# Two products of a gated delta-rule recurrence, computed as 64x64 tiles of TensorE

## The reference, cut to what matters

```python
def step(M, inp):
    q_t, k_t, v_t, b_t, g_t = inp
    M = M * jnp.exp(g_t)[..., None, None]
    Mk = jnp.einsum('bhd,bhdv->bhv', k_t, M)
    M = M + jnp.einsum('bhd,bhv->bhdv', k_t, (v_t - Mk) * b_t[..., None])
    o_t = jnp.einsum('bhd,bhdv->bhv', q_t, M)
    return (M, o_t)
```

## Time and profile before

| | |
|---|---|
| Three runs | 2204.56, 2207.28 and 2207.43 us, median 2207.28 us |
| Profiled execution, span | 2206.9 us |
| Mean granted TensorE clock | 0.989 of full speed |
| Busy: PE, PEld | 2103.0 us (95%), 1734.9 us (79%) |
| Busy: DVE, ACT, POOL | 1242.6 us (56%), 988.4 us (45%), 814.4 us (37%) |

### The profile page before, as it was taken

The page is one execution under the profiler, slowest core; times in us unless marked ns, Lnnn a source line. Parts: engine busy times, 40 slices in busy tenths (PEclk is TensorE's granted clock), DMA queues, the critical chain, the costliest instruction groups (busy, mean ns, idle before and its releaser), DMA issues.

```text
span 2206.9 us, 37731 instructions
## 1 busy us (share of the span) xinstructions
PE 2103.0 (95%) x12418; PEld 1734.9 (79%) x12418; DVE 1242.6 (56%) x2160; ACT 988.4 (45%) x3083; POOL 814.4 (37%) x1169
## 2 busy tenths in 40 slices
PE   5899999999999999999999999999999799999999
PEld 4688888888988888888888888888898665757574
DVE  5656565656666656566565656565666544343434
ACT  2455454546364646454555545464636331212111
POOL 2254453535353636353545445353535200000000
PEclk9899999999999999999999999999999989999999
DMA  2011111101010101010101111111102340403020
GB/s 93 15 34 26 29 36 21 31 21 35 22 38 14 38 19 38 14 38 15 37 21 31 29 24 36 21 31 21 36 21 63 125 128 10 115 16 109 19 57 19
DMA packets 220091, 85.37 MB, mean 39 GB/s; under 512 B 138320, under 2 KB 204240, under 8 KB 219280
## 3 DMA queue, kind: packets, MB, share of 16 engines
q1 hardware_dynamic: 220048, 84.83, 15.2%
HBM read 57.28 MB, written 27.53 MB: 38 GB/s over the span
## 4 chain that ended last, share of the span: by engine, by line
PE 72%; issue 12%; DVE 9%; ACT 3%; POOL 2%; DMA 1%; POOLq 0%; DVEq 0%; SPq 0%; ACTq 0%
PE bank L515 27%; PE bank L683 5%; PE bank L670 5%; PE bank L771 4%; PE bank L708 3%; PE bank L635 3%; PE bank L728 2%; PE bank L735 2%; PE bank L714 2%; PE bank L719 2%; PE bank L734 2%; PE bank L702 2%; DVE vT L1316 2%; PE bank L588 1%; PE bank L834 1%
## 5 line engine op out<-in xcount | busy, mean ns | idle before, releaser
L515 PE MATMUL bank<-x_hi,w_hi 128*128 128x512 f32 x1024 | 422.6, 413 | 18.3 <-DVE w_lo L1263 11.6
L515 PE MATMUL bank<-x_hi,w_lo 128*128 128x512 f32 x1024 | 409.5, 400 | 0.0
L515 PE MATMUL bank<-x_lo,w_hi 128*128 128x512 f32 x1024 | 408.5, 399 | 0.0
L515 PEld LDWEIGHTS bank<-x_hi,w_hi 128*128 128x128 f32 x1024 | 194.0, 189 | 60.0 <-issue 16.2
L515 PEld LDWEIGHTS bank<-x_hi,w_lo 128*128 128x128 f32 x1024 | 193.8, 189 | 36.7
L515 PEld LDWEIGHTS bank<-x_lo,w_hi 128*128 128x128 f32 x1024 | 194.5, 190 | 31.3
L1316 DVE SCALAR_TENSOR_TENSOR qT<-bank,cw,qT 128x511 f32<-128x511 f32 (+2 forms) x192 | 143.4, 747 | 82.7 <-ACT qT L954 78.1
L1316 DVE SCALAR_TENSOR_TENSOR vT<-bank,cw,vT 128x511 f32<-128x511 f32 (+2 forms) x192 | 143.2, 746 | 44.8 <-ACT vT L954 40.3
L1707 POOL TENSOR_TENSOR o_rstd<-o_ms,minus_half 128x4 f32<-128x4 f32 x64 | 70.7, 1104 | 258.1 <-DVE o_ms L1395 258.1
L1739 POOL TENSOR_TENSOR rstd<-ve,mhalf 128x1 f32<-128x1 f32 x32 | 17.4, 543 | 387.6 <-DVE ve L1479 387.6
L1114 ACT ACTIVATE o_tmp<-bank 128x128 f32<-128x128 f32 x256 | 67.4, 278 | 201.5 <-PE bank L735 201.5
(11 more groups left out here) (219 smaller groups left out, 4860.6 us busy)
## 6 DMA issues: line engine op xcount, KB each, us to landing
w_raw<-in_w_heads SPq DMA_DIRECT2D x64, 256.0 KB, 2.8
o_d<-og SPq DMA_DIRECT2D x64, 256.0 KB, 2.6
o_raw<-o_d SPq DMA_DIRECT2D x16, 1024.0 KB, 6.1
x_in<-in_x SPq DMA_DIRECT2D x16, 256.0 KB, 3.4
blkN_d<-nT SPq DMA_DIRECT2D x64, 64.0 KB, 2.0
t<-blkT_d SPq DMA_DIRECT2D x64, 64.0 KB, 2.4
wo_raw<-in_w_out SPq DMA_DIRECT2D x4, 1024.0 KB, 7.9
x_res<-in_x SPq DMA_DIRECT2D x16, 256.0 KB, 2.7
```

The lines of the kernel that those rows point to most:

```text
L515: last = mm(bank[bk][:, :], w[:, kind % 2, d, :], xx[:, d, b * S:(b + 1) * S], start=(n == 0), stop=(n == 3 * ND - 1))
```

## The change

The two products, L714 and L719, use only the blocks that matter: L714 takes the 64 rows of the early half and the 64 columns of the late half of `nT`, and L719 takes the late half of `tT` both ways. Each matmul's weights become 64x64, its moving operand 64 rows x 128 columns, and its result the upper 64 partitions of the bank. The copy to `vv` and the subtraction from `w1` work on those 64 partitions. The memsets, their three waits, and TensorE's wait for them go. An instruction that only adds 1 to a semaphore is put on TensorE before each of the two products, behind the wait for the copy.

```diff
+EARLY, LATE = slice(0, P // 2), slice(P // 2, P)
@@ semaphores: x2_only goes, "pe" comes to held @@
@@ TensorE, one chunk of the recurrence @@
                     pe.wait_ge(w1_done, 4 * h + c + 1)
-                    pe.wait_ge(x2_only, 2 * h + 2)
+                    hold(pe, "pe")
                     for b in range(B):
-                        last = mm(grid(2)[:, b, :], nT[:, b, c, :], w1[:, c % 2, b, :], start=True, stop=True)
+                        last = mm(grid(2)[LATE, b, :], nT[EARLY, b, c, LATE], w1[EARLY, c % 2, b, :], start=True, stop=True)
                     last.then_inc(v_mm, 1)
                     ahead(fill[2])
                     pe.wait_ge(vv_done, 4 * h + c + 1)
+                    hold(pe, "pe")
                     for b in range(B):
-                        last = mm(grid(3)[:, b, :], tT[:, b, c, :], vv[:, b, :], start=True, stop=True)
+                        last = mm(grid(3)[LATE, b, :], tT[LATE, b, c, LATE], vv[LATE, b, :], start=True, stop=True)
@@ ScalarE @@
-                    fn(vv[:, :, :], grid(2), ACT.Copy).then_inc(vv_done, 1)
+                    fn(vv[LATE, :, :], grid(2)[LATE], ACT.Copy).then_inc(vv_done, 1)
@@ VectorE @@
-                    tt(w1[:, c % 2, :, :], w1[:, c % 2, :, :], grid(3), ALU.subtract).then_inc(w_done, 1)
+                    tt(w1[LATE, c % 2, :, :], w1[LATE, c % 2, :, :], grid(3)[LATE], ALU.subtract).then_inc(w_done, 1)
@@ GpSimd @@
-                pool.wait_ge(x1_done, 4 * h + 4)
-                pool.wait_ge(x0_done, 4 * h + 4)
-                pool.wait_ge(qg_done, 3 * h + 3)
-                hold(pool, "pool")
-                for i in range(2):
-                    s = i * P // 2
-                    memset(nT[s:s + P // 2, :, :, s:s + P // 2], 0.0).then_inc(x2_only, 1)
-                    pool.wait_ge(x2_only, 2 * h + i + 1)
-                    if i == 0:
-                        hold(pool, "pool")
```

More of the change, by code:

```diff
@@ L287, in layer @@
         sem(n) for n in ("blkT_zero", "blkN_out", "blkN_in", "inv_set", "sub_step", "blkT_out", "t32_in", "tT_done", "t32_done"))
-    x0_done, x1_done, y_mrg, y_copied, z_mrg, merged, x2_only = (
-        sem(n) for n in ("x0_done", "x1_done", "y_mrg", "y_copied", "z_mrg", "merged", "x2_only"))
+    x0_done, x1_done, y_mrg, y_copied, z_mrg, merged = (
+        sem(n) for n in ("x0_done", "x1_done", "y_mrg", "y_copied", "z_mrg", "merged"))
     ks_mm, rhs_done, w1_mm, w1_done, v_mm, vv_done, tv_mm, w_done, sg_done, s_mm, s_done = (
@@ L315, in layer @@
     heads_over = [sem(f"heads_over_{e}") for e in ("pe", "act", "dve", "pool")]
-    held = {"dve": sem("dve_held"), "pool": sem("pool_held"), "sp": sem("sp_held")}
+    held = {"pe": sem("pe_held"), "dve": sem("dve_held"), "pool": sem("pool_held"), "sp": sem("sp_held")}
     def hold(engine, name):
```

## The result

The changed kernel takes 2231.49 us (median of 4 runs, 2226.84 to 2234.40) against 2207.02 us (median of 4 runs of the kernel before, the three above and one more). The ratio is 1.0112, with a 95% interval of 1.0097 to 1.0126: slower by 24.5 us. The profiled execution has a span of 2231.1 us, 24.2 more than before, and a time of 2233.03 us.

What follows compares the result with a forecast made beforehand. TensorE, 95% busy, bounds it, with the product-copy chain as long as the fill beside it. Added instruction +8.4 less shorter loads 6.0 gives +2.4; with shape changes +9.7 to +44.8, middle +27: 2206.9 + 27, 2234 us; range 2200 to 2258.

Steps and rivals of the forecast that it cites:

- The stall at the change of shape: Between fill and products, four shape changes a chunk, 240 in 15 heads, drain TensorE; sum between +9.7 and +44.8 us.
- the middle between two ends 35 us apart: Shape-change cost taken midway between +9.7 us (load merely cannot overlap) and +44.8 us (load waits for the record's end): +27.
- Entry: From fill to product, the product begins later: +0.04 to +0.19 us in 105 products, -0.04 to +0.11 in 15.
- Exit: From product back to fill, the fill's load finishes later: +0.10 to +0.28 us in each of 120 products.
- The added instruction: Semaphore increment ahead of L714 and L719: 0.08 us in 105 products, 8.4 us; nothing beside a draining array.
- Memsets, copy and subtraction at 0: Removing GpSimd's 32 memsets and cutting copy L1108 and subtraction L1408 to 64 partitions gains 0 on the path.
- What the waits hide: Exits after L719 partly covered by existing waits: 5.9 us off the lower end, 10.4 us off the upper.
- the last head: The head without fill: little of the added instruction's cost is counted there, and no shape changes.
- Rival 1: At the shape changes, no stall: 2206.9 + 2.4, about 2209.5 us; chance 0.25.
- rival 3: Within a small-tile product, loads run in series, 0.05 us longer per pair, 48 us more: 2282 us; chance 0.06.
- rival 2: At the products' joints, shorter first load (6.0 us) and earlier results (4.8 us) make it faster: 2196 us; chance 0.19.
- The 0.4 us that the prediction set between span and time: Profiled span of 2206.9 us against the timed median of 2207.28; 0.4 us treated as lying around the span.

Runs made afterwards that it cites:

- full_held: Changed kernel with both products 128x128 again and memsets back, added instruction kept before both, VectorE subtracting on 64 partitions: 2215.50 us, ratio 1.0040.
- full_free: Changed kernel with both products 128x128 again, memsets back, no added instruction, VectorE subtracting on 64 partitions: 2209.36 us, ratio 1.0009 to the kernel before.
- full_last: Changed kernel with 128x128 products in the last head alone, memsets in all heads: 2228.21 us, ratio 1.0092 to the kernel before.
- cols_only: Changed kernel with both products on all 128 rows but 64 columns, memsets back: 2227.44 us, ratio 1.0091 to the kernel before.

## Why the prediction was right, step by step

- Direction and size were right: 2234 forecast, 2231.49 measured, +27 against +24.5. The stall at the change of shape exists, in both splits of the array. Its price was not read from any row: the prediction took the middle between two ends 35 us apart, and that the runs fell there is partly luck. The Trainium skill's sentence that a change of tiling mode drains the TensorE (TensorEngine Tiling (Array Packing), Key Properties) agrees with the traces; what it costs, about 0.09 us beyond the streaming and the load that can't be hidden, is the runs' to say.
- Entry: forecast, as the middle, a product that begins 0.12 later; measured in chunk 1, 0.32 + 0.05 = 0.37 behind the start of the fill matmul against 0.25, so 0.12. In the mean of 15 heads the distance between the first matmul records of L708 and L714 grew by 0.09, that between L714 and L719 by 0.29 in chunks 1 to 3 (0.23 in chunk 0, where a register operation went), with one exit and one entry in it. Exit: forecast 0.19 in the middle, measured 0.29 less some 0.10 for the entry, 0.19.
- The added instruction: 0.08 forecast, 0.07 seen in `full_held`, 6.1 us in sum where 8.4 stood. Under a draining array it should cost nothing, as forecast: a load 0.11 behind the copy's end, as in `full_held`, would start before the 0.32 are over. No run shows this apart.
- Memsets, copy and subtraction at 0: right.
- Two terms were mis-sized, in opposite directions. What the waits hide: forecast, between the two ends, about 8 us; in the profiles the 15 periods from one head's first L708 to the next grew by 1.3 us each, 19.4 in sum, where entries and exits alone make 0.28 x 120 = 33.6. So 14 us are hidden. The prediction read only the first gap behind the fill, up to L728 or the transposes. But the chain waits again behind L728, and in chunk 2 of the head shown L734 starts 2.93 us behind L719 as before, although L728 starts 0.08 later: in chunks 1 and 2 the next L708 follows L719 after 7.00 us, as before (6.99), in chunk 0 after the 6.83 that `full_free` has with 128x128 products. So all three exits are covered whole, where the prediction read 0.09 for chunk 0, the whole for chunk 1 and 0.11 for chunk 2. Behind chunk 3 the way to the next head's first L708 is even 0.31 shorter, where 0.21 was read as cover. And the last head, to which I gave nothing because it has no fill, cost 5.9 us of the profiled execution through the clock. The forecast of 27 is near the 24.5 partly because these two nearly cancel, and that is luck. The 20 us of stall alone would have been 2227, which is what `full_last` (2228) and `cols_only` (2227) show.
- Rival 1 (no stall) falls with the entries and exits in the traces, rival 3 (loads in series) with the pace in a group, which is still 0.11. Of rival 2, the earlier result is there, with 0.08 less from the first load to ScalarE's copy, but buried under the stall. I had not listed the clock as a rival.
- The 0.4 us that the prediction set between span and time is 1.7 to 2.8 us in the executions that give both (1.9 in the profiled one of the changed kernel). This changes the forecast little, since it adds to a measured span and compares with medians.

## What to carry to other kernels

A smaller tile doesn't make a single stream of matmuls faster when their moving operand is as long as before. It brings a stall at each change of shape, so look at what stands between the products: here full-size fill, four changes a chunk. The gain lies in using several tiles at once, and it pays for the changes only if the copies out of PSUM don't eat it: 0.42 us saved a product, 0.16 given back by each split copy or subtraction. A wait already there behind a joint hides it; ask for each joint apart, and look for stretches without fill, where the clock can fall.

## What the runs showed of the hardware

- After 128*128 matmuls, the first load of a 64*64, 64*128 or 128*64 matmul starts 0.31 to 0.33 us after the start of the last 512-column one, against 0.15 to 0.22 without a change of shape. The way back costs about the same 0.09 and the whole load of 0.10 besides. This is measured between these fill matmuls and these products only.
- 64*64 matmuls on two column tiles of the same rows run side by side: eight records in 0.59 us up to the next fill load, against 1.01 on one tile, with no cost for going from tile to tile.
- ScalarE and VectorE read 64 partitions of PSUM and write to the other 64 of SBUF, VectorE with its other operand there too. Two instructions of 256 elements take 0.15 to 0.16 more than one of 512.
- TensorE's granted clock fell to its lower level for part of the last head with both products on 64*64 tiles (mean 0.83) or on 64 rows (0.87), and with L714 alone small (0.82), and stayed at 1.00 there with 128*128, with 128*64, and with L719 alone small.
